# One boundary's work in another order on four engines, with re-shaped transfers, an earlier first slot and a moved loop turn, in a two-layer attention kernel

## The chip, the cores and the metric

The kernel runs on one core of a Trainium2 chip. The metric is the device time of one execution in microseconds (us), from loading the inputs to the last store of the output. Five engines run their own instruction streams in order: PE (matmuls), DVE and ACT (elementwise work and reductions), POOL (a slower elementwise engine) and SP, which here only issues DMAs. They are tied together by semaphores: an instruction increments one when it is done, another engine's stream waits until the count is reached. A stream never overtakes its own waiting instruction.

## What is computed

Eight images of 128 channels and 64 x 64 pixels pass through two layers.

```
# layer 0: wavelet split of x into four bands (32 x 32 each)
ll = (x1 + x2 + x3 + x4) / 2 ; lh, hl, hh = the three differences / 2
# low band: sparse attention, 8 heads of 16, N = 1024
q, k, v = qkv(ll);  q, k = q/|q|, k/|k|
attn = clip(q k^T * scale);  keep the 512 largest of each row, rest -1e9
ll_out = group_norm(proj(softmax(attn) v))
# three high bands: depthwise 3x3, group_norm, silu, 1x1 (384x384), group_norm
high = h + alpha * gn2(pw(silu(gn1(dw(h)))))
x_rec = inverse wavelet(ll + ll_out, high)
out = x + 0.1 * x_rec;  out = out + 0.1 * gn(w2 gelu(gn(w1 out)))
# layer 1: full attention over N = 4096 pixels with 16-wide q and k
q, k, v = Wq x + bq, Wk x + bk, Wv x + bv
x = gamma * (Wo (v softmax(q k^T / 4)^T) + bo) + x
```

## The kernel before, in words

The eight images form a pipeline of depth two. A stretch called `slots(b, l0, l1)` runs the eight heads of layer 0 of image b together with the eight chunks (512 queries each) of layer 1 of image b - 1. Between two such stretches stands `between(f, n, fin, opn)`: it finishes layer 0 of image f (`fin`: projection, group norms, ffn, and q, k, v of layer 1) and opens image n (`opn`: wavelet bands, q, k, v of layer 0, the convolutions of the high bands). There are nine such calls; the text calls them boundaries. The one that finishes image 0 is the first of eight that finish an image, and the fourth finishes image 3, at 2878 to 3050 us. The order of work on every engine is written out by hand, as a list of calls inside each engine's `between` and `slots`; every call contains its own waits. The same name on two engines (say `ffn1(3)`) is the two engines' share of one step.

**The turn of the loop.** Images 1 to 6 run in a hardware loop, `Fori(1, images - 1)`, whose body is `slots(b)` followed by `between(b, b + 1)`. The boundary after image 0 stands ahead of the loop and the last slots and boundary behind it. The loop turns back five times, from the end of a boundary to the start of the next slots.

**The end of the slots.** DVE masks the last exponentials of head 7 (line 1403), then copies the head's result out of PSUM (`head_out`, line 1456, tile OT; the rows 16, 48, 80 and 112 of OT hold the sums of the softmax). SP's `store_head` gathers those sums into OD (128 x 8, line 281) and stores the head to scrO (line 283); DVE's `sums` takes the reciprocal of OD (line 1462) and SP stores it to scrD (line 287). `load_done` reads all heads and reciprocals back as OC and OB, heads 0 to 6 first, head 7 at the boundary (lines 271, 276). Before `store_head` of head 7 SP issues that first `load_done` and, once head 7's masks are complete, the first half of the next image's x (`load_x`, line 243).

**The boundary.** `heads_out` (DVE, line 1632) multiplies OC by OB; `proj` (PE, line 647) projects; group norm 0 goes PE `group`, DVE `variance`, POOL `power`, PE `ungroup`, DVE `scales`; ACT `band0`, DVE `add0` give the new x (X1); `ffn1` (lines 682, 1029, 1691), group norm 3, `gelu` (line 1037), `ffn2` (lines 692, 1043, 1698), group norm 4, `norm2` and `add2` follow. Then `qk1`, `part1` (q and k of layer 1 split into three bf16 parts, PT1; the last is DVE line 1716, semaphore p12) and `values1`. Beside it, for the image that opens: POOL makes the bands out of x (`pairs`, `bands`, lines 1940 to 1968); `values0` (line 752), `qk0` (line 726) and `conv` (line 778) run on PE, the nine `taps` per band on DVE; `squares`, `clamp` and POOL's `norms` (a pow over 128 x 128, line 1975) and `repeat` (line 1981) give 1/|q| and 1/|k|; `spread` (PE, line 767) turns them and `normal` (DVE, line 1730) applies them; `part0` splits into bf16 parts; `silu` (line 1127), `points` (line 793) and `band` finish the high bands.

PE works in PSUM bank 4 for `qk0`, `values0`, `squares` and `spread`, one at a time.

**SP at the boundary.** `store_planes` writes the parts of layer 0 to scr0 (line 262, 12 DMAs of 256 KB), `load_head` reads the first three heads (line 255). Then X1 is stored to scrX (line 362, 2 MB), PT1 to scr1 (line 365, 3 x 256 KB, each row cut into its four places j), and q and k of layer 1 are read back as QP1 and KP1 (line 371, 7 DMAs, 1.5 MB); last the three high bands go to scrL (line 375).

**The first slot.** PE's `first` runs scores 2 to 7 of head 0 (line 428), then the 32 maxima products of chunk 0 (line 485), each in bank 4; DVE reduces each (line 1469) before the next one may start. The first of them waits for QP1 and KP1. ACT evicts the scores (line 905) and counts, for each of 1024 rows, the scores above a threshold (line 915); DVE's `update` (line 1272) moves the threshold after each round. In DVE's `first` the first four updates stand after maxima 5, 8, 13 and 17.

## Time and profile before

| | us |
|---|---|
| median of 3 runs | 6520.9 (6519.24 to 6528.7) |
| the profiled execution | 6521.32 |
| its span, first to last instruction | 6519.5 |
| PE busy | 4871.5 (75%) |
| DVE busy | 4702.5 (72%) |
| ACT busy | 4550.5 (70%) |
| POOL busy | 402.4 (6%) |
| mean granted clock of PE | 0.87 |

A profile is one execution on the chip. Times in it count from the span's start. Busy shares are averages over stretches with different limits. Idle time in brackets stands just before an instruction, with what ended it; it costs only where the engine is the one that everybody waits for. PEclk is PE's granted clock as a share of full speed. The DMA share is the mean busy share of the 16 DMA engines, so one engine at work all the time is 0.06.

### The profile page before, as it was taken

The numbers are of one execution on the slowest core, as the hardware profiler recorded it, in microseconds if no ns is written. First come the engines' busy times: TensorE is split into PE (matmuls) and PEld (weight loads), VectorE is DVE, ScalarE is ACT, GpSimd is POOL, SyncE is SP. The second block draws the span as 40 slices with busy tenths as digits, with TensorE's granted clock in tenths as the row PEclk, the third lists the DMA queues.
The fourth block names the chain that finished last, engine by engine and source line by source line (L and its number), as shares of the span: only waits on it lengthen the run. The fifth ranks groups of instructions, "written<-read, shape, count | busy, mean of one in ns | idle before, by whom it ended". The sixth has DMA issues, their size and how long they took to land.

```text
span 6519.5 us, 90843 instructions
## 1 busy us (share of the span) xinstructions
PE 4871.5 (75%) x30180; PEld 3041.3 (47%) x30180; DVE 4702.5 (72%) x8351; ACT 4550.5 (70%) x6907; POOL 402.4 (6%) x133
## 2 busy tenths in 40 slices
PE   4343688875888668875888758876788758884788
PEld 2000356542556335652556425553456425562566
DVE  3666588965998578975989659875898758983443
ACT  4884589945997469955999469964899459982223
POOL 3001100020000300011000200002000200000000
PEclk7555799986999879987999869997899869996899
DMA  1001100011001200011000110011000110001000
GB/s 59 6 9 44 64 13 14 13 49 66 13 18 40 74 12 16 15 51 64 13 16 35 41 50 18 16 52 64 9 18 13 48 64 15 18 33 36 9 7 12
DMA packets 97485, 199.95 MB, mean 31 GB/s; under 512 B 33960, under 2 KB 38952, under 8 KB 91336
## 3 DMA queue, kind: packets, MB, share of 16 engines
q1 hardware_dynamic: 96968, 193.57, 8.7%
q8 instruction: 261, 4.28, 0.3%
q14 instruction: 256, 2.10, 0.1%
HBM read 110.61 MB, written 82.05 MB: 30 GB/s over the span
## 4 chain that ended last, share of the span: by engine, by line
DVE 36%; issue 20%; PE 17%; ACT 11%; DMA 7%; POOL 5%; SPq 3%; DVEq 1%; ACTq 0%; POOLq 0%
DVE MX L1469 10%; ACT work L915 6%; PE PS L519 6%; DVE M L1325 6%; DVE arena L1403 6%; PE PS L485 4%; DVE work L1317 3%; DVE work L1285 3%; DVE work L1309 3%; DMA KP<-scr 3%; POOL RN L1975 3%; ACT work L933 2%; PE PS L457 2%; DMA scr<-arena 2%; SPq L262 1%
## 5 line engine op out<-in xcount | busy, mean ns | idle before, releaser
L915 ACT ACTIVATE work<-arena,T 128x1024 bf16<-128x1024 f32 x1792 | 2039.9, 1140 | 355.1 <-DVE T L1272 323.9
L519 PEld LDWEIGHTS PS<-V,work 128*128 128x128 f32 x16384 | 2017.7, 195 | 120.1 <-ACT work L940 29.2
L519 PE MATMUL PS<-V,work 128*128 128x129 f32 x16384 | 2045.8, 279 | 22.4 <-ACT work L940 22.4
L1469 DVE TENSOR_REDUCE MX<-PS 128x1 f32<-128x512 f32 x2048 | 1407.6, 687 | 743.3 <-PE PS L485 732.1
L485 PE MATMUL PS<-KP,QP 96*128 96x512 bf16 x2048 | 854.4, 417 | 646.3 <-DVE MX L1469 432.1
L940 ACT ACTIVATE work<-PS 128x1024 f32<-128x1024 f32 x1024 | 1039.7, 1015 | 406.4 <-PE PS L503 406.3
L485 PEld LDWEIGHTS PS<-KP,QP 96*128 96x128 bf16 x2048 | 200.9, 98 | 1215.5 <-DVE MX L1469 951.3
L1403 DVE SCALAR_TENSOR_TENSOR arena<-PS,work 128x1024 f32<-128x1024 f32 x512 | 624.6, 1220 | 194.1 <-ACT work L933 194.0
L503 PE MATMUL PS<-QP,KP 99*128 99x512 bf16 x2048 | 621.4, 385 | 60.1 <-ACT work L940 37.0
L905 ACT ACTIVATE arena<-PS 128x1024 f32<-128x1024 f32 x512 | 520.9, 1017 | 199.5 <-PE PS L428 198.4
L1325 DVE MAX8 M<-work 128x8 f32<-128x1024 f32 x512 | 625.5, 1222 | 3.0
L933 ACT ACTIVATE work<-PS 128x1024 f32<-128x1024 f32 x512 | 520.3, 1016 | 139.6 <-PE PS L457 136.3
L457 PE MATMUL PS<-work 99*128 99x512 bf16 x1024 | 336.9, 413 | 240.5 <-DVE arena L1403 185.4
L428 PE MATMUL PS<-work 96*128 96x512 bf16 x1024 | 362.5, 441 | 200.4 <-ACT arena L905 161.5
L1309 DVE TENSOR_SCALAR work<-arena,T 128x1024 f32<-128x1024 f32 x512 | 382.9, 748 | 23.7 <-DVE M L1325 5.7
L1317 DVE TENSOR_SCALAR work<-work,FL 128x1024 uint32<-128x1024 uint32 x512 | 376.4, 748 | 4.5
L915 ACT ACTIVATION_READ_ACCUMULATOR work<-arena,T 128x1 f32 x1792 | 343.4, 192 | 0.0
L1285 DVE TENSOR_SCALAR_CACHE_REDUCE work<-arena,T 128x1024 bf16<-128x1024 f32 x256 | 325.0, 1272 | 0.0
L503 PEld LDWEIGHTS PS<-QP,KP 99*128 99x128 bf16 x2048 | 182.3, 98 | 261.6 <-ACT work L940 89.5
L468 PE MATMUL PS<-arena,VT 128*17 128x256 f32 x4096 | 302.4, 408 | 0.0
L1940 POOL TENSOR_TENSOR work<-work 128x1024 f32<-128x1024 f32 x8 | 22.3, 2788 | 4383.2 <-DMA work<-in_x 4383.2
L457 PEld LDWEIGHTS PS<-work 99*128 99x128 bf16 x1024 | 66.0, 99 | 430.5 <-DVE arena L1403 355.0
(179 smaller groups left out, 3981.6 us busy)
## 6 DMA issues: line engine op xcount, KB each, us to landing
scr<-work SPq DMA_DIRECT2D x96, 256.0 KB
work<-scr SPq DMA_DIRECT2D x128, 192.0 KB, 2.7
work<-in_x SPq DMA_DIRECT2D x16, 1024.0 KB, 5.8
arena<-in_x SPq DMA_DIRECT2D x8, 2048.0 KB, 11.3
scrX<-arena SPq DMA_DIRECT2D x8, 2048.0 KB, 9.2
XR<-scrX SPq DMA_DIRECT2D x64, 256.0 KB, 2.7
out<-YO SPq DMA_DIRECT2D x64, 256.0 KB, 2.0
scrL<-work SPq DMA_DIRECT2D x24, 512.0 KB, 6.8
```

The costliest lines, as they stand in the source:

```text
L457: last = mm(PS[:, c, :], kp(h)[0:KA, 128 * mt:128 * mt + 128], qp(h)[0:KA, 512 * c:512 * c + 512], start=True, stop=True)
L485: mm(PS[:, 4, :], QP1[0:KS, c * 512 + 128 * i:c * 512 + 128 * i + 128], KP1[0:KS, 512 * w:512 * w + 512], start=True, stop=True).then_inc( ...
L503: last = mm(PS[:, 2 + t, :], KP1[0:KA, 128 * mt:128 * mt + 128], QP1[0:KA, j * 512:j * 512 + 512], start=True, stop=True)
L519: last = mm(PS[:, 5 + i // 2, 136 * (i % 2):136 * (i % 2) + 129], P1[:, (16 * j + k) % 3, t, 128 * i:128 * i + 128], V1[:, mt, :], start=( ...
L915: A(JKA[:, m % 2, :], scores(h, i), ACT.Sign, scale=-1.0, bias=T[:, h % 2, i:i + 1], accum_out=CA[:, h % 2, i:i + 1]).then_inc(s["ca"], 1)
L933: A(JA[:, mt % 2, :], bank2(0), ACT.Exp, scale=0.25).then_inc(s["e"], 1)
L940: A(P1[:, (16 * j + k) % 3, :, :].rearrange("p t n -> p (t n)"), PS[:, 2:4, :].rearrange("p a n -> p (a n)"), ACT.Exp, scale=0.25).then_in ...
L1309: cp.did(V.tensor_scalar(JD[:, c, :], scores(h, i), T[:, h % 2, i:i + 1], None, ALU.subtract))
L1317: cp.did(V.tensor_scalar(JDu[:, c, :], JDu[:, c, :], FL[:, h % 2, i:i + 1].bitcast(u32), None, ALU.bitwise_xor))
L1325: cp.did(V.max(M8[:, h % 2, i, :], JD[:, c, :]))
L1403: V.scalar_tensor_tensor(scores(h, mt), bank2(0), 0.0, JA[:, mt % 2, :], ALU.is_ge, ALU.mult)\
L1469: V.reduce_max(MX[:, c % 2, i, w:w + 1], PS[:, 4, :], AX.X).then_inc(s["mr"], 1)
```

## The change

Five things change.

1. Transfers. PT1 goes to scr1 row by row as it lies, and QP1 and KP1 are read with twelve DMAs of 16 rows (six pairs) in place of seven; scr1 becomes [3, 128, 1024]. The stores and loads now stand ahead of scrX's store. For heads 0 to 6 the gather of the sums is four DMAs, one per row of OT, in place of one. Head 7 has no gather: DVE takes the reciprocal of all of OT into a new tile OX, and SP stores its four rows.
2. SP issues the first `load_done` and the first half of the next x in head 7's slot right after the sums of head 6, ahead of the store of chunk 7.
3. The first slot. DVE's thresholds are updated between the first maxima (after 0, 3, 7, 11), and the four counts of round 2 and both their updates move from `search(0)` into `first`.
4. The loop's body is now the boundary `between(b - 1, b)` followed by `slots(b)`, so the loop turns back from the end of the slots to the start of a boundary; one boundary stands behind the loop.
5. The order of the calls in `between` on PE, ACT, DVE and POOL: the first value tile ahead of group norm 0, the second ahead of `ungroup(3)`, the spreads in one run ahead of the points, the first part of the second half's convolution ahead of ffn1; `repeat` ahead of `power(1)`.

The diff, cut to its core (the moved calls of `between` are shown for PE and, in part, for DVE, ACT and POOL):

```diff
@@ -103,7 +103,7 @@
-scr1 = nc.dram_tensor("scr1", [3, 32, N1], bf16, kind="Internal").ap()
+scr1 = nc.dram_tensor("scr1", [3, 128, N0], bf16, kind="Internal").ap()
...
@@ -263,10 +264,10 @@
...
     if first:
-        sp.wait_ge(s["od"], (b * NH + NH - 1) * 80)
+        sp.wait_ge(s["od"], b * OUTS + (NH - 1) * 128)
         rows, heads = slice(0, 112), slice(0, NH - 1)
     else:
-        sp.wait_ge(s["od"], (b + 1) * (NH * 80))
+        sp.wait_ge(s["od"], (b + 1) * OUTS)
         rows, heads = slice(112, 128), slice(NH - 1, NH)
...
@@ -278,13 +279,21 @@
...
     sp.wait_ge(s["o"], b * NH + h + 1)
-    sp.dma_start(OD[:, h % 2, :], OT[HD:128:32, h % 2, :].rearrange("q (j e) -> q j e", e=8)).then_inc(s["od"], 16)
+    if h < NH - 1:
+        for q in range(4):
+            sp.dma_start(OD[32 * q:32 * q + 32, h % 2, :],
+                         OT[32 * q + HD:32 * q + HD + 1, h % 2, :].rearrange("p (j e) -> p j e", e=8))\
+                .then_inc(s["od"], 16)
     for q in range(4):
-        sp.dma_start(scrO[h, :, 256 * q:256 * q + 256], OT[32 * q:32 * q + HD, h % 2, :]).then_inc(s["od"], 16)
+        sp.dma_start(scrO[h:h + 1, :, 256 * q:256 * q + 256].rearrange("h d n -> (h d) n"),
+                     OT[32 * q:32 * q + HD, h % 2, :]).then_inc(s["od"], 16)

...
     sp.wait_ge(s["rd"], b * NH + h + 1)
-    sp.dma_start(scrD[h:h + 1, :].rearrange("h (p e) -> (h p) e", e=8), ODR[:, h % 2, :]).then_inc(s["odr"], 16)
+    if h < NH - 1:
+        sp.dma_start(scrD[h:h + 1, :].rearrange("h (p e) -> (h p) e", e=8), ODR[:, h % 2, :]).then_inc(s["odr"], 16)
+    else:
+        sp.dma_start(scrD[h].rearrange("(q n) -> q n", q=4), OX[HD:128:32, :]).then_inc(s["odr"], 16)

...
@@ -317,12 +326,6 @@
...
             load_parts(b)
-        if l0 and h == NH:
-            load_done(b, True)
-            if more:
-                sp.wait_ge(s["p"], (b + 1) * (NH * NT))
-                sp.sem_inc(s["free"], 1)
-                load_x(b + 1, 0)
         if head(h):
...
@@ -341,6 +344,12 @@
...
             load_head(h + 3)
+        if l0 and h == NH - 1:
+            load_done(b, True)
+            if more:
+                sp.wait_ge(s["p"], (b + 1) * (NH * NT))
+                sp.sem_inc(s["free"], 1)
+                load_x(b + 1, 0)
         if chunk(h):
...
@@ -358,17 +367,16 @@
...
     if fin:
+        sp.wait_ge(s["p12"], f + 1)
+        for a in range(3):
+            sp.dma_start(scr1[a], PT1[:, a, :]).then_inc(s["scrw1"], 16)
+        sp.wait_ge(s["scrw1"], (f + 1) * 48)
+        for j, (tq, tk) in enumerate(TERMS):
+            for w, (t, dst) in enumerate(((tq, QP1), (tk, KP1))):
+                sp.dma_start(dst[16 * j:16 * j + 16].rearrange("p (j n) -> p j n", j=4),
+                             scr1[t].rearrange("(j s) n -> s j n", s=32)[16 * w:16 * w + 16]).then_inc(s["qp1"], 16)
         sp.wait_ge(s["x2"], (f + 1) * 4)
         sp.dma_start(scrX[bass.ds(f, 1)].rearrange("a c n -> c (a n)"), X1).then_inc(s["xs"], 16)
-        sp.wait_ge(s["p12"], f + 1)
-        for a in range(3):
-            sp.dma_start(scr1[a].rearrange("s (j n) -> j s n", j=4), PT1[:, a, :]).then_inc(s["scrw1"], 16)
-        sp.wait_ge(s["scrw1"], (f + 1) * 48)
-        q, k = scr1[:, 0:16, :], scr1[:, 16:32, :]
-        for dst, src in ((QP1[0:32], q[0].unsqueeze(0).to_broadcast([2, 16, N1])), (KP1[0:32], k[0:2]),
-                         (QP1[32:64], q[1].unsqueeze(0).to_broadcast([2, 16, N1])), (KP1[32:64], k[0:2]),
-                         (QP1[64:96], q[0:3:2]), (KP1[64:80], k[2]), (KP1[80:96], k[0])):
-            sp.dma_start(dst, src).then_inc(s["qp1"], 16)
     if opn:
...
@@ -381,10 +389,10 @@
...
 slots(0, True, False)
-between(0, 1, True, True)
 with sp.Fori(1, images - 1) as b:
+    between(b - 1, b, True, True)
     slots(b, True, True)
-    between(b, b + 1, True, True)
+between(images - 2, images - 1, True, True)
 slots(images - 1, True, True, False)
...
...
@@ -746,7 +754,7 @@
...
         else:
-            pe.wait_ge(s["qn"], n * 4 + 4)
+            pe.wait_ge(s["ssm"], n + 1)
         for m in range(4):
...
@@ -759,7 +767,7 @@
...
             pe.wait_ge(s["re"], n + 1)
-            pe.wait_ge(s["ssm"], n + 1)
+            pe.wait_ge(s["vt"], n * 2 + 2)
         else:
...
@@ -796,14 +804,15 @@
...
     proj(1)
+    values0(0)
     group(0)
-    values0(0)
+    qk0(0)
     ungroup(0)
     conv(0, 0, 0)
-    qk0(0)
     conv(0, 0, 1)
+    conv(0, 0, 2)
     qk0(1)
-    conv(0, 0, 2)
+    conv(0, 1, 0)
     qk0(2)
...
@@ -816,15 +825,15 @@
...
     ffn1(10)
+    qk0(3)
     ffn1(11)
     ffn1(12)
-    qk0(3)
     ffn1(13)
...
     group(3)
-    conv(0, 1, 0)
+    values0(1)
     ungroup(3)
...
@@ -834,23 +843,22 @@
...
     ffn2(5)
+    ffn2(6)
     group(1)
-    ffn2(6)
+    ffn2(7)
+    spread(0)
     ungroup(1)
-    spread(0)
     spread(1)
-    ffn2(7)
+    group(4)
     spread(2)
+    ungroup(4)
+    spread(3)
     points(0, 0)
-    spread(3)
     points(0, 1)
-    group(4)
-    values0(1)
     points(1, 0)
-    ungroup(4)
     points(1, 1)
+    values1(0)
     points(2, 0)
-    values1(0)
     points(2, 1)
...
...
@@ -1143,16 +1151,16 @@
...
     values0(0)
+    qk0(0)
     band0()
-    qk0(0)
     square(0)
...
     ffn1(2)
+    ffn1(3)
     qk0(2)
-    ffn1(3)
     ffn1(4)
...
@@ -1162,59 +1170,59 @@
...
     qk0(3)
+    square(3)
     ffn1(11)
     ffn1(12)
-    square(3)
     ffn1(13)
...
     ffn1(15)
+    values0(1)
     gelu(0)
...
     gelu(3)
+    conv(0, 0)
+    ffn2(0)
     gelu(4)
     gelu(5)
-    ffn2(0)
-    conv(0, 0)
+    ffn2(1)
     gelu(6)
     gelu(7)
-    ffn2(1)
     ffn2(2)
     ffn2(3)
-    conv(0, 1)
     ffn2(4)
     ffn2(5)
+    ffn2(6)
+    ffn2(7)
+    conv(0, 1)
     silu(0)
...
     part0(0, 0)
-    ffn2(6)
-    ffn2(7)
+    part0(0, 1)
+    norm2(0)
+    norm2(1)
+    points(0, 0)
     part0(1, 0)
-    part0(0, 1)
-    points(0, 0)
+    points(0, 1)
     part0(1, 1)
-    values0(1)
-    points(0, 1)
-    norm2(0)
+    norm2(2)
+    norm2(3)
     points(1, 0)
-    norm2(1)
-    norm2(2)
+    values1(0)
     points(1, 1)
-    norm2(3)
     points(2, 0)
-    values1(0)
+    points(2, 1)
     qk1()
...
     values1(1)
-    points(2, 1)
     values1(2)
     part1(1)
+    values1(3)
     band(0)
-    values1(3)
     values1(4)
+    values1(5)
     band(1)
-    values1(5)
     values1(6)
...
...
@@ -1452,13 +1460,18 @@
...
         if h >= 1:
-            dve.wait_ge(s["od"], (b * NH + h) * 80)
+            dve.wait_ge(s["od"], b * OUTS + h * 128)
         V.tensor_copy(OT[:, h % 2, :], PS[:, 7, 0:256]).then_inc(s["o"], 1)
+        if h == NH - 1:
+            dve.wait_ge(s["o"], (b + 1) * NH)
+            V.reciprocal(OX[:, :], OT[:, h % 2, :]).then_inc(s["rd"], 1)

...
             return
-        dve.wait_ge(s["od"], (b * NH + h + 1) * 80)
+        if h == NH - 1:
+            return
+        dve.wait_ge(s["od"], b * OUTS + h * 128 + 128)
         V.reciprocal(ODR[:, h % 2, :], OD[:, h % 2, :]).then_inc(s["rd"], 1)
...
...
@@ -1504,30 +1517,54 @@
...
         centre(0, 1)
-        for k in range(24):
+        update(0, 0, 0)
+        for k in range(3):
             maxima(0, k)
-            if k in (5, 8, 13, 17):
-                g = (5, 8, 13, 17).index(k)
-                update(0, g // 2, g % 2)
+        update(0, 0, 1)
+        for k in range(3, 7):
+            maxima(0, k)
+        update(0, 1, 0)
+        for k in range(7, 11):
+            maxima(0, k)
+        update(0, 1, 1)
+        for i in range(4):
+            count(0, 2, 4 + i)
+            maxima(0, 11 + i)
+        update(0, 2, 0)
+        update(0, 2, 1)
+        for k in range(15, 30):
+            maxima(0, k)

     def search(h):
-        count(h, 2, 4)
-        maxima(h, 24)
+        if h >= 1:
+            count(h, 2, 4)
+        if h >= 1:
+            maxima(h, 24)
         mask(h - 1, 3)
-        count(h, 2, 5)
-        maxima(h, 25)
-        count(h, 2, 6)
-        maxima(h, 26)
...
@@ -1790,81 +1827,81 @@
...
     add0(2)
+    taps(1, 0)
     add0(3)
-    taps(2, 0)
-    taps(1, 0)
-    taps(2, 1)
+    taps(1, 1)
+    conv(0, 0)
     ffn1(0)
+    taps(1, 2)
     ffn1(1)
     ffn1(2)
-    taps(1, 1)
-    conv(0, 0)
     ffn1(3)
-    taps(1, 2)
+    taps(2, 0)
     ffn1(4)
+    taps(2, 1)
     ffn1(5)
...
     ffn1(8)
-    taps(1, 3)
     ffn1(9)
+    taps(2, 2)
     ffn1(10)
-    taps(1, 4)
+    taps(2, 3)
     ffn1(11)
...
     moments(3)
+    taps(2, 4)
     clamp()
     variance(3)
+    taps(2, 5)
+    taps(1, 3)
+    scales(3)
+    taps(1, 4)
     taps(1, 5)
-    taps(2, 2)
-    scales(3)
-    taps(2, 3)
-    taps(2, 4)
     taps(1, 6)
-    taps(2, 5)
     taps(1, 7)
+    taps(2, 6)
     taps(1, 8)
-    taps(2, 6)
+    conv(0, 1)
     taps(2, 7)
-    conv(0, 1)
-    taps(2, 8)
+    ffn2(0)
     conv(1, 0)
     conv(1, 1)
+    taps(2, 8)
+    ffn2(1)
     conv(2, 0)
+    ffn2(2)
     conv(2, 1)
+    ffn2(3)
     moments(1)
+    ffn2(4)
     variance(1)
-    ffn2(0)
+    ffn2(5)
+    ffn2(6)
+    ffn2(7)
+    normal(0)
+    moments(4)
     scales(1)
-    ffn2(1)
-    normal(0)
-    ffn2(2)
-    ffn2(3)
-    ffn2(4)
     normal(1)
-    ffn2(5)
+    variance(4)
+    normal(2)
+    normal(3)
+    scales(4)
+    points(0, 0)
+    add2(0)
     part0(1, 0)
-    normal(2)
-    ffn2(6)
+    points(0, 1)
+    part0(1, 1)
     part0(2, 0)
-    ffn2(7)
-    points(0, 0)
-    normal(3)
-    moments(4)
-    part0(1, 1)
-    points(0, 1)
     part0(2, 1)
-    variance(4)
-    scales(4)
     points(1, 0)
+    add2(1)
     points(1, 1)
-    add2(0)
-    add2(1)
+    add2(2)
     points(2, 0)
-    add2(2)
     add2(3)
...
...
@@ -2000,8 +2037,8 @@
...
     norms()
+    repeat()
     power(f, n, fin, opn, 1)
-    repeat()
     power(f, n, fin, opn, 4)
...
@@ -2012,13 +2049,14 @@
...
 between(0, 0, False, True)
-between(0, 1, True, True)
 with pool.Fori(1, images - 1) as b:
-    between(b, b + 1, True, True)
+    between(b - 1, b, True, True)
+between(images - 2, images - 1, True, True)
 between(images - 1, images, True, False)
...
 DSET = 15
+OUTS = (NH - 1) * 128 + 64

...
```

## Rows read from the trace of the kernel before

**Rows 1.** Waits, all engines: waiter <- releaser: us in total, times, longest us.
```profile
PE PS L485 <- DMA KP<-scr: 172.5, 7, 38.6
...
PE PS L428 <- issue: 32.0, 5, 6.5
```

**Rows 2.** Chain of work, 2870 to 3060 us: start, us, what.
```profile
2880.08 9.39 DMA work<-in_x
...
3024.09 25.56 DMA KP<-scr
```

**Rows 3.** SP timeline, DMA issues of a slot and the fourth boundary.
```profile
2785.81 1.86 SPq L283 DMA_DIRECT2D scrO<-OT  x4
...
2793.89 0.34 SPq L287 DMA_DIRECT2D scrD<-ODR  x1
...
2881.14 2.35 SPq L283 DMA_DIRECT2D scrO<-OT  x4
2890.66 0.34 SPq L287 DMA_DIRECT2D scrD<-ODR  x1
...
2892.08 0.58 SPq L276 DMA_DIRECT2D work<-scrD  x1
2978.90 13.97 SPq L262 DMA_DIRECT2D scr<-work  x12
...
3002.96 5.67 SPq L365 DMA_DIRECT2D scr<-arena  x3
3020.25 0.69 SPq L371 DMA_DIRECT2D QP<-scr  x1
```

**Rows 4.** Windows: busy PE, PEld, DVE, ACT, POOL; PEclk, DMA share, GB/s.
```profile
3004.00:3006.00 2.00, 0.51 (x5) 0.32 (x3) 0.00 (x0) 1.55 (x2) 0.00 (x0) 1.00 1.06 424
...
3014.00:3016.00 2.00, 0.79 (x3) 0.13 (x2) 0.00 (x0) 1.11 (x2) 0.00 (x0) 0.50 0.26 100
...
3038.00:3040.00 2.00, 0.00 (x0) 0.00 (x0) 0.00 (x0) 0.00 (x0) 0.00 (x0) 0.50 0.14 57
```

**Rows 5.** PE timeline, fourth boundary: start, us, engine, line, what [idle <-releaser].
```profile
2896.34 3.71 PE L647 MATMUL PS<-work,w_proj 128*128 128x512 f32 x4 [18.14 <-DVE work L1632]
...
2904.36 2.08 PE L752 MATMUL PS<-w_qkv,work 128*128 128x128 f32 x8 [1.87 <-POOL work L1958]
...
2921.10 11.32 PE L682 MATMUL PS<-arena,w 128*128 128x512 f32 x26
...
3011.00 1.03 PE L428 MATMUL PS<-work 96*128 96x512 bf16 x2 [6.49 <-issue]
...
3049.70 0.61 PE L485 MATMUL PS<-KP,QP 96*128 96x512 bf16 x1 [21.75 <-DMA KP<-scr]
```

**Rows 6.** DVE timeline, fourth boundary; last row: the last boundary's first maxima.
```profile
2878.27 0.42 DVE L1456 COPY OT<-PS 128x256 f32<-128x256 f32 x1 [0.27 <-PE PS L468]
...
2894.51 1.77 DVE L1632 TENSOR_TENSOR work<-work 128x1024 f32<-128x1024 f32 x1 [3.88 <-DMA work<-scrD]
...
2999.55 1.23 DVE L1716 TENSOR_TENSOR arena<-arena 128x1024 bf16<-128x1024 f32 x1 [0.72 <-ACT arena L1066]
...
6018.67 0.69 DVE L1469 TENSOR_REDUCE MX<-PS 128x1 f32<-128x512 f32 x1 [41.63 <-PE PS L485]
```

**Rows 7.** POOL timeline: first boundary's start, fourth boundary's pow.
```profile
627.75 2.79 POOL L1940 TENSOR_TENSOR work<-work 128x1024 f32<-128x1024 f32 x1 [517.62 <-DMA work<-in_x]
...
2942.16 21.66 POOL L1975 TENSOR_TENSOR RN<-SSM,mhalf 128x128 f32<-128x128 f32 x1
```

**Rows 8.** ACT timeline, fourth boundary: the silus, the last count.
```profile
2966.23 3.50 ACT L1127 ACTIVATE work<-work,SHH,SCH 128x1024 f32<-128x1024 f32 x3 [3.79 <-DVE SHH L1676]
...
3032.83 1.13 ACT L915 ACTIVATE work<-arena,T 128x1024 bf16<-128x1024 f32 x1
```

**Rows 9.** The page, part 6, x loads: count, KB each, median us to landing.
```profile
work<-in_x SPq DMA_DIRECT2D x16, 1024.0 KB, 5.8
```

**Rows 10.** PE timeline, first boundary: its first maxima matmul.
```profile
786.26 0.61 PE L485 MATMUL PS<-KP,QP 96*128 96x512 bf16 x1 [27.07 <-DMA KP<-scr]
```

41 lines of the change are left out of this document (28 added, 13 removed).

## The prediction, written before the change was run

> **What bounds the kernel now.** I read the list of waits first, then the chain of work around one boundary between images (2870 to 3060 us, the fourth of eight), then the timelines of SP, PE, DVE, ACT and POOL there, and last the windows for what the DMA engines did. The waits name two PE stalls that happen only at boundaries: the first maxima matmul (line 485) waits 172.5 us in seven boundaries for the KP1/QP1 loads, and the first score matmul (line 428) sits 6.5 us five times with nothing to wait for, once per turn of the loop [rows 1]. The chain shows how much of a boundary is transfer: 9.39 us for the next image's x and 25.56 us for the KP1 loads [rows 2]; the scr1 stores, issued from 3002.96, hold the loads back until 3020.25 [rows 3]. The windows explain both. While SBUF row tiles move whole (3004 to 3006), the share of the 16 DMA engines is 1.06 at 424 GB/s; while the scr1 stores drain (3014 to 3016) it is 0.26, four engines' worth; during the KP1/QP1 loads (3038 to 3040) it is 0.14 at 57 GB/s, about two engines' worth [rows 4]. The stored pattern leads with 4 (j), most of the loads lead with 2. So width follows the leading dimension, and PE idles 21.75 us behind two engines [rows 5].
>
> **Where one loop boundary spends its time.** In us of the fourth boundary: head 7 copied out at 2878.69, heads_out starts 2894.51 [rows 6], x has landed at 2889.47 [rows 2], the low band is ready about 2904.3, ffn1 starts 2921.10 [rows 5], the pow of the norms runs 2942.16 to 2963.82 [rows 7], silu starts 2966.23 [rows 8], the layer-1 parts (p12) are complete at 3000.78 [rows 6], the first maxima matmul runs at 3049.70 [rows 5]. From there 32 maxima ping-pong between PE and DVE, and nothing overtakes them. The first maxima is therefore the milestone; its gain is the image's gain.
>
> **Part 1, transfers of the head output and of x.** Before, the x half (1 MB) is issued at 2880.08, just ahead of head 7's stores, and these (issued by 2883.49) let the reciprocal and its store go only at 2890.66 [rows 2, 3]. After, the x half is issued as soon as the last mask is done, some 2873.1: it lands 5.8 us (the page's median, [rows 9]) later or somewhat sooner, at 2878 to 2879. x is 10.5 to 11 us earlier, so the low band is ready near 2893.2 instead of 2904.3. Head 7's four stores go out at about 2878.8 onto quiet queues; SP is done with them by 2880.7 and they land by 2882.2 (1.5 us later, an estimate from the small gaps on quiet queues). The gather OD and the small reciprocal are gone; one reciprocal of 128x256 on DVE replaces them (0.42 us if it runs like the copy of that size in [rows 6], 1.4 us if its cost per element is larger; both are over before SP has issued the four stores). The two loads then follow, and as before heads_out starts 1.85 us after the last one is issued [rows 3, 6]. That gives heads_out at about 2885.2, 9.3 us earlier.
>
> **Part 2, the order of the boundary**, walked with the durations of the same trace. PE does proj (3.7 us from 2896.34, [rows 5]), then the value tile first: it waits for the low band until 2893.2, 2.1 us [rows 5], and the group matmul behind it starts at 2895.2, behind its own turn by some 2 us. DVE's variance then follows without POOL beside it, and ungroup ends near 2898.4, 9.6 us earlier. The convolution of the second half now stands ahead of ffn1 (2.74 us more, 1 us of qk less): ffn1 starts about 2914.2, 6.9 us earlier. ffn1 is paced by DVE: 16 statistics of 0.6 us and 5 taps of 1.2 us, 15.5 us in all; before, it was one tap less and one statistic more, much the same. taps(2,4) ahead of clamp costs 1.2 us, the second value tile takes the place of 4.5 us of convolution before ungroup: gelu starts 7.5 us earlier and the pow at 2936.5, 5.7 us earlier. The pow is unchanged at 21.66 us [rows 7]. Repeat (1.88 us) now runs ahead of the band norm's power, and normal(0) and moments(4) stand before scales(1) on DVE: silu starts at about 2963.6, only 2.6 us earlier. Behind it the order pays. All four spreads and the value tile are done while ACT runs silu (3.50 us, [rows 8]), and the six pointwise products run back to back (6 x 2.7 us, one value tile between); before, three spreads, a value tile and ffn2 stood between them. p12 comes at 2991.8, 9.0 us earlier. PE ends the values about 2995 and ACT about 2996.5. The six head loads are no limit: twelve plane stores take 13.97 us of SP [rows 3], now from 2969.2, and land about 2988.2.
>
> **Part 3, the loop turn.** It moves from before the scores to before heads_out, where PE waits anyway. The 6.49 us [rows 5] go from PE's path. SP now turns between the store of the sums and the loads. No row shows SP's turn; its bounds are 0 and PE's 6.5. A late heads_out is half hidden by the 2 us wait for the low band, so at most 3.2 us a boundary are lost; I take half, 1.6, in five boundaries: 8 us.
>
> **Part 4, scr1.** SP is free at p12 and nothing of scrX is in front. Three stores at 1.16 us each (13.97 / 12, [rows 3]) and about 2.5 us to land: 2997.8. Twelve loads at 0.62 us each (the first took 0.69, [rows 3]) are issued by 3005.2 and land 1.85 us later, about 3007 (9.3 us after the first issue). The other bound is the rate of the four-engine rows: 1.5 MB at 100 GB/s, 15 to 16 us, about 3014 [rows 4]. I take the first, since both sides of each load now lead with 16. PE meanwhile runs the eight scores: they start at ACT's pace near 2996.5 and end at 3011.5. So PE, no longer the load, is late, and the first maxima matmul goes at 3011.5: 38.2 us earlier. The scrX store moves behind the loads; its readers are the XR loads and the eviction of head 1, some 70 us later, which hide it.
>
> **Part 5, first slot.** The thresholds no longer wait for maxima, so ACT idles less. But ACT was ahead anyway; the ping-pong sets the end, and the four DVE counts only change place. A small cost appears: update(0,0,1) stands after three maxima (4.2 us), and ACT's eighth count ends 6.1 us after the last score (before: 3033.96 [rows 8] against 3027.95, where PE's 21.75 us of idling begin [rows 5]). DVE waits 1.8 us, with PE's next maxima behind it. Net per loop boundary: 38.2 - 1.8 = 36.4 us. The others differ by fractions from the fourth; I use 36.1.
>
> **The other boundaries.** In the first one x was early already (POOL starts at 627.75, 3.8 us after the head copy [rows 7]), so value tile and convolution ahead of their old places cost: p12 2.3 us later. Its first maxima goes from 786.26 after 27.07 us of idling [rows 10] to about 761.6: 24.7 less 1.8, 22.9 us. In the last, without a next image, heads_out comes 6.5 us earlier (896 KB no longer ahead of the stores), and p12 to first maxima shrinks from 41.0 us (DVE idled 41.63, [rows 6]) to 14.0 us: 33.5 us together. In the slots SP issues three more gathers per head (1.9 us); the sums wait until 2793.89, 6.2 us after the last store of 2785.81 was issued [rows 3], which hides it at no cost; without that cover it costs DVE up to 1.9 us a head.
>
> **Sum:** 22.9 + 6 x 36.1 + 33.5 - 8 = 265 us. The profiled execution took 6521.3 us (span 6519.5); the median of 6520.9 stands 0.4 below. 6521 - 265 = 6256 us.
>
> What a page says of the width: the Trainium skill, DMA: Bandwidth & Descriptors, section "Why a DMA increments its semaphore by 16 and not by 1", lets a transfer run on the largest number of engines up to 16 that divides the leading sizes of both sides. By that rule it is 4 and 2 engines before, and the trace agrees (0.26, 0.14 [rows 4]). By the same rule it is 16 for the new stores and loads, which no row shows, and the sum would be the one above; with rival B it would be wrong.
>
> **Rivals.**
> A, the loads are wide but slow, at 100 GB/s for 16 target partitions (the four-engine rate, [rows 4]). The loads then land 3014 to 3016.5 and eat the 1.8 us too: about 1.5 us in each of six boundaries, 2 in the first, 7 in the last: 18 us, 6274 us. For it: no row here fills 16 partitions with much data. Against: that rate came with four engines. A page speaks for it: SBUF — State Buffer, section "Door 1: The DMA port swizzle" of the Trainium skill, says that bandwidth goes by the SBUF ports that the partitions reach, 27.2 GB/s each; by that page 16 partitions reach 4, an estimate of 109 GB/s and 14 us for 1.5 MB. No run so far shows it.
> B, the transfers don't get wider, so the change doesn't do what it says. 3 stores and loads then take about 35 us from p12: maxima near 3027, 22.7 us gained in six boundaries, 9 in the first, 13 in the last: 158 us, 6363 us. Against: head loads and x with 96 and 128 leading rows do fill the engines.
> C, the order gives nothing: the wait for the low band ahead of group and the pow ahead of spreads and silu eat what x and heads_out give, p12 stays put. 9 us in six boundaries: 54 us less, 6310 us. For it: silu gains only 2.6 us in my walk.
> D, slower than before: the gathers of heads 0 to 6, now four transfers each out of one partition, land late and DVE waits in sums, with masks and maxima behind it. Price: the 56 heads would have to lose 265 / 56 = 4.7 us each, so gathers would have to land 4.7 + 4.3 = 9 us after the last store instead of within 6.2. Beyond 9 us the kernel is slower; at 10 it takes 6575 us. Against: 128 pieces of 32 bytes per head, as before.
>
> **How the numbers follow.** Forecast 0.55, A 0.25 (6274), C 0.10 (6310), B 0.07 (6363), D 0.03. The forecast's own range is 6228 (no SP turn, each boundary 3 us better) to 6280. The range 6228 to 6315 takes in A and C. Faster by over 0.2% (13 us, about what a measurement of this kernel can tell from no change): all but D and a sliver, 0.96; same 0.01; slower 0.03.
>
> **What would show it.** After: no wait of line 485 on KP loads over 3 us except in the last boundary; a DMA share well above 0.14 right after p12; 8 to 10 us from head copy to heads_out; the wait before line 428 without its 6.5 us; silu start to p12 28 us instead of 34.5; pow unchanged at 21.66 and starting about 58 us after the head copy instead of 63.5; DVE's sums without a wait in heads 0 to 6. A first maxima that still waits 5 to 10 us on loads says A, 15 or more B; p12 more than 112 us after heads_out says C (I expect 106.6; before, 106.3). What would make it wrong: a wait in the new order that my walk of four queues missed, multiplied by six.

## The result, and the profile after

The changed kernel takes 6239.9 us (median of 4 runs, 6235.4 to 6247.7) against 6520.8 us: ratio 0.9568, 95% interval 0.9552 to 0.9585, 281 us less. The forecast was 6256 (range 6228 to 6315). The profiled execution took 6235.5 us (span 6233.7), so between the two profiled executions lie 285.8 us. Medians here are of fast runs: one of the four runs of the kernel with the scr1 transfers alone took 6938.4 us at a granted clock of 0.69 and isn't counted.

Page of the changed kernel, busy times and the chain by engine:

```profile
PE 4879.6 (78%) x30180; PEld 3049.5 (49%) x30180; DVE 4693.0 (75%) x8351; ACT 4554.4 (73%) x6907; POOL 401.2 (6%) x133
...
DVE 32%; PE 21%; issue 19%; ACT 18%; POOL 4%; DMA 3%; SPq 2%; DVEq 0%; ACTq 0%; POOLq 0%
```

In its list of waits (total, times, longest) the KP loads are down from 172.5 us to 16.9, of which 15.4 stand in the last boundary, and no row is left for the turn of the loop at the first score [rows 1]:

```profile
DVE MX L1482 <- PE PS L493: 537.8, 699, 18.4
...
PE PS L655 <- DVE work L1669: 80.3, 8, 12.4
...
PE PS L493 <- DMA KP<-scr: 16.9, 2, 15.4
```

SP at the fourth boundary (start, duration, what was issued). The x half goes out 5 us ahead of the head copy (which ends at 2777.83), then come the head's stores and the sums; the loads for heads_out are issued at 2782.97 and 2783.42. 2.2 us lie between the two pairs, the wait for the stores and SP's loop turn:

```profile
2772.32 0.35 SPq L244 DMA_DIRECT2D work<-in_x  x1
...
2777.86 2.27 SPq L288 DMA_DIRECT2D scrO<-OT  x4
2780.17 0.58 SPq L296 DMA_DIRECT2D scrD<-OX  x1
2782.97 0.32 SPq L272 DMA_DIRECT2D work<-scrO  x1
2783.42 0.54 SPq L277 DMA_DIRECT2D work<-scrD  x1
```

SP at the end of the same boundary, where p12 is complete at 2891.51: three stores, 4.5 us, and twelve loads at 0.47 us from start to start.

```profile
2891.54 1.32 SPq L372 DMA_DIRECT2D scr<-arena  x3
2896.04 0.33 SPq L376 DMA_DIRECT2D QP<-scr  x1
...
2901.09 0.43 SPq L376 DMA_DIRECT2D KP<-scr  x1
2901.81 0.37 SPq L379 DMA_DIRECT2D scrX<-arena  x1
```

PE there. Scores run from 2894.43, the last at 2910.51, and the first maxima matmul follows with no wait. In the row of before it waited 21.75 us [rows 5]:

```profile
2894.43 0.60 PE L436 MATMUL PS<-work 96*128 96x512 bf16 x2
...
2910.51 1.03 PE L436 MATMUL PS<-work 96*128 96x512 bf16 x2 [1.21 <-ACT arena L913]
2911.34 0.63 PE L493 MATMUL PS<-KP,QP 96*128 96x512 bf16 x1
```

Windows of the same stretch (last two columns: share of the 16 DMA engines and GB/s; the one before is PE's granted clock). The loads have all engines busy, but move only 115 GB/s, where [rows 4] had 424 with the same share:

```profile
2892.00:2894.00 2.00, 1.61 (x15) 1.46 (x14) 0.00 (x0) 2.00 (x5) 0.00 (x0) 1.00 1.03 354
...
2902.00:2904.00 2.00, 0.79 (x3) 0.13 (x2) 0.17 (x1) 1.38 (x3) 0.00 (x0) 0.50 1.05 115
2904.00:2906.00 2.00, 0.58 (x2) 0.00 (x0) 0.00 (x0) 2.00 (x5) 0.00 (x0) 0.50 1.07 115
```

Only the last boundary, where no scores stand in front, still shows how long the loads take: first issue at 5720.25, first maxima at 5734.57, 14.3 us.

```profile
5720.25 0.33 SPq L376 DMA_DIRECT2D QP<-scr  x1
```
```profile
5734.57 0.59 PE L493 MATMUL PS<-KP,QP 96*128 96x512 bf16 x1 [15.36 <-DMA KP<-scr]
```

Times of the milestones behind the end of the last head copy (us), worked out from the timelines (heads_out and silu: their start; p12: the end of the last part; first maxima: the start of the matmul); "fourth" is the boundary of the working:

| | heads_out | silu | p12 | first maxima |
|---|---|---|---|---|
| first, before / after | 8.3 / 7.2 | 79.4 / 85.3 | 115.3 / 113.5 | 161.9 / 133.3 |
| fourth, before / after | 15.8 / 8.0 | 87.5 / 81.6 | 122.1 / 113.7 | 171.0 / 133.5 |
| last, before / after | 12.5 / 5.9 | none | 89.4 / 81.4 | 130.4 / 99.2 |

The first maxima gains 28.6 us in the first boundary, 36.4, 38.1, 37.5, 37.7, 39.4 and 38.0 in the next six and 31.2 in the last: 286.9. Before the first boundary 3.0 us are lost, the slots lose 0.5 and the end gains 2.3: 285.7 of the 285.8. The gain is all at the boundaries.

### The profile page after: what moved, and what is told of

Same layout as the page of the kernel before. It is cut to its first block, busy times and chain, and to the rows that moved or that the text cites. A ratio compares the mean times of both kernels' runs of the same rounds, so it can differ in the third digit from the quotient of the medians.

```text
span 6233.7 us, 91139 instructions
## 1 busy us (share of the span) xinstructions
PE 4879.6 (78%) x30180; PEld 3049.5 (49%) x30180; DVE 4693.0 (75%) x8351; ACT 4554.4 (73%) x6907; POOL 401.2 (6%) x133
## 4 chain that ended last, share of the span: by engine, by line
DVE 32%; PE 21%; issue 19%; ACT 18%; POOL 4%; DMA 3%; SPq 2%; DVEq 0%; ACTq 0%; POOLq 0%
ACT work L923 10%; DVE MX L1482 9%; PE PS L527 6%; DVE M L1333 5%; DVE arena L1411 5%; PE PS L493 4%; ACT work L941 3%; DVE work L1325 3%; POOL RN L2012 3%; DVE work L1293 3%; DVE work L1317 2%; ACT work L948 2%; PE PS L465 2%; PE PS L801 2%; PE PS L786 1%
## 5 line engine op out<-in xcount | busy, mean ns | idle before, releaser
L1317 DVE TENSOR_SCALAR work<-arena,T 128x1024 f32<-128x1024 f32 x512 | 383.1, 748 | 19.7 <-DVE M L1333 0.5
## 6 DMA issues: line engine op xcount, KB each, us to landing
scrX<-arena SPq DMA_DIRECT2D x8, 2048.0 KB, 14.5
```

## The experiments

Kernels are told by what they change against the changed kernel, unless the text says otherwise. One warning on size: the four runs of the changed kernel spread over 12 us, those of one experiment (two queues) over 30. The experiments ran on four chips, each beside the kernel before (6522.7 to 6524.8 us there) but not beside the changed kernel. A difference under some 10 us between two medians is not explained here unless a row of the trace carries it.

**The scr1 transfers alone**, put into the kernel before:

```diff
-scr1[a].rearrange("s (j n) -> j s n", j=4) <- PT1[:, a, :]      # leads with 4
+scr1[a] <- PT1[:, a, :]                                         # leads with 128
-QP1[0:32], KP1[0:32], ... <- scr1 (leads 2)                     # 7 loads
+for j: QP1[16j:16j+16], KP1[16j:16j+16] <- scr1 (leads 16)      # 12 loads, scrX behind them
```

> The kernel before with the scr1 transfers of the change alone (row-shaped stores, twelve loads of 16 rows, the scrX store behind them); order, loop turn, x and first slot as before. My theory (the wide transfers are hidden behind the scores, and the stall of the first maxima was theirs alone): in each boundary the wait of the first maxima on the KP1 loads goes, 27.1 us in the first, 20 to 22.5 in the next six, 23 in the last (p12 to first maxima 41.0 to 17.7 us), together some 180 us, 6341 us; p12 stays about 122 us behind the head copy. Rival (the 37.5 us of a loop boundary are mainly the order and the loop turn): gain below 100 us, over 6420 us, with a wait of 10 us or more left before the first maxima. In neither the loads' rate rises: about 115 GB/s with all 16 engines busy, not 424.

Measured 6331.2 us (ratio 0.9706, interval 0.9687 to 0.9726), 191.5 less than the kernel before on the same chip. No wait on the loads is left but the last boundary's 15.95 us, and p12 stays where it was or comes up to 2 us later (122.2 to 124.2 us behind the copy in the loop, 122.0 to 122.7 before). In the five boundaries with a turn of the loop, p12 to first maxima is 23.4 to 25.2 us: the turn of the loop still stands there, and scores, not loads, are last. Two thirds of the whole gain are this one edit.

**The next image's x and the load of seven heads back at their old place:**

> The changed kernel with the next image's first x half and the load of seven finished heads at their old place (ahead of the last head's stores instead of a head earlier). Theory: x lands 10.5 us later, heads_out some 4 us later (the half moves in front of the head's stores), p12 6 to 7 us later in six boundaries and 3 in the last: 6275 to 6285 us. Rival (x is not on the path with the new order): heads_out decides alone, p12 4 us later or less, under 6262 us.

Measured 6323.2 us (ratio 0.9695, interval 0.9679 to 0.9711): 83 us are lost, twice the expectation. DVE and PE of its fourth boundary (head copy ended 2802.76):

```profile
2818.35 3.23 DVE L1669 TENSOR_TENSOR work<-work 128x1024 f32<-128x1024 f32 x1 [13.80 <-DMA work<-scrD]
```
```profile
2821.63 3.78 PE L655 MATMUL PS<-work,w_proj 128*128 128x512 f32 x4 [19.36 <-DVE work L1669]
2829.76 2.07 PE L760 MATMUL PS<-w_qkv,work 128*128 128x128 f32 x8 [4.35 <-POOL work L1995]
```

heads_out is 7.6 us later (15.6 against 8.0) and takes 3.23 us. In the changed kernel it took 1.23 there, but 1.2 to 3.3 over the eight boundaries, with GpSimd's passes beside it in both kernels; what makes the difference is open. The value tile, which stands first in the new order, waits 4.35 us for the late low band (1.48 in the changed kernel) with the group matmul behind it. ffn1 starts 46.4 behind the copy instead of 33.1, and p12 comes 8 to 17 us later in the six boundaries between the first and the last, as much as heads_out (7.6 to 9.3) or more. So the 7.8 us by which heads_out came earlier are the place of x and of the seven heads' load, not the head's own transfers. The two were moved together. In the last boundary there is no next x, and there the load's place alone makes 5.1 us (heads_out at 11.0 instead of 5.9).

**The old transfers of a head's sums:**

```diff
-for q in range(4): OD[32q:32q+32, ...] <- OT[32q+HD:32q+HD+1, ...]    # heads 0 to 6
+OD[:, ...] <- OT[HD:128:32, ...]                                       # one gather, all 8 heads
-V.reciprocal(OX, OT[:, h % 2, :]); scrD[h] <- OX[HD:128:32, :]         # last head
```

> The changed kernel with the old transfers of a head's sums (one gather of three-partition pieces, small reciprocal, one row store, also for the last head). Theory: in the slots the one gather costs or saves nothing; at the boundary the last head's sums go out a landing and a small reciprocal later, heads_out 2 to 3 us later than 8.0 behind the head copy, of which half is hidden by the wait for the low band: 6248 to 6262 us. Rival (the 7.8 us by which heads_out came earlier are this edit's own): heads_out at 14 us or more, 6285 us or more.

6235.1 us (ratio 0.9557, interval 0.9542 to 0.9571), no loss at all. heads_out is 2 to 3 us later as expected (9.9 to 10.8), yet in the fourth boundary ffn1 starts earlier (31.4 for 33.1) and p12 is at 110.6 for 113.7. In the last boundary the changed kernel's form is worth 3.6 us at p12 (81.4 for 85.1). The slots take the same 583.0 us, so the gathers of heads 0 to 6 cost nothing. Its PE at the fourth boundary, and the changed kernel's:

```profile
2788.66 3.72 PE L646 MATMUL PS<-work,w_proj 128*128 128x512 f32 x4 [12.55 <-DVE work L1655]
2792.22 1.05 PE L751 MATMUL PS<-w_qkv,work 128*128 128x128 f32 x8
...
2795.92 7.99 PE L777 MATMUL PS<-PAD,diag 128*128 128x512 f32 x18
```
```profile
2787.10 3.78 PE L655 MATMUL PS<-work,w_proj 128*128 128x512 f32 x4 [9.76 <-DVE work L1669]
2792.36 2.07 PE L760 MATMUL PS<-w_qkv,work 128*128 128x128 f32 x8 [1.48 <-POOL work L1995]
...
2797.63 9.15 PE L786 MATMUL PS<-PAD,diag 128*128 128x512 f32 x18
```

With heads_out later the value tile has nothing to wait for and runs in 1.05 us instead of 2.07, the convolutions in 7.99 instead of 9.15: PE's granted clock is back at 1.00 from 15.6 us behind the copy, in the changed kernel from 22.2. The earlier heads_out of the changed kernel was paid back by a wait and a half clock.

**The old order of the boundary's work** on all four engines:

> The changed kernel with the old order of the boundary's work on PE, ACT, DVE and POOL, everything else of the change kept. Theory (the order is worth what stands between heads_out and p12, 106.3 before and 105.7 after): 0.6 us a boundary at p12 and 0.6 more up to the end of the scores, 6244 us at most; heads_out 8.0 us behind the head copy, p12 within 115. Rival (the order carries the 8.4 us by which p12 comes earlier, since only it uses the early x): p12 at 120 to 122 us behind the copy, 6285 to 6295 us.

6230.6 us (ratio 0.9553, interval 0.9537 to 0.9569; 6227.3 to 6231.5, below every run of the changed kernel). So the order of the change gains nothing. Whether it costs something isn't shown: the medians are 9 us apart, but the first maxima of the two profiled executions differ by 2.6 us over all eight boundaries. Silu starts at 76.3 to 78.0 (80.1 to 81.8 in the changed kernel), 2.4 us behind the end of the pow instead of 5.3, and p12 is at 110.1 to 114.0 although it has the old 34 to 36 us from silu to p12.

**Silu's scales ahead of repeat and the first spread again**, then also **one pointwise product between the spreads**:

```diff
 norms(); -repeat(); power(1); +repeat()                       # GpSimd
 -normal(0); -moments(4); scales(1); +normal(0); +moments(4)   # DVE
 ffn2(7); +ungroup(1); spread(0); -ungroup(1); ...             # PE
 spread(2); +points(0, 0); ungroup(4); spread(3); -points(0, 0)   # second kernel only
```

> The changed kernel with the scales of the band norm ahead of repeat, of the first spread and of normal(0) on GpSimd, PE and DVE, as before the change; the spreads still in one run behind it. Theory: silu starts 2.4 us behind the end of the pow, as before (78.8 instead of 81.7 us behind the head copy), but the four spreads in one run still end after it and at half clock: points start no earlier than about 87, p12 at most 1 us earlier, 6231 to 6240 us. Rival (silu alone holds up the points): points and p12 3 us earlier, 6215 to 6222 us.

> As the one before it, and the first pointwise product stands between the third and the fourth spread on PE. Theory (the run of small matmuls, 128 columns each, is what the half clock of 10 us comes from and goes with): points start at 83 to 84 instead of 87.9, the granted clock is back at 1.0 some 5 us earlier, p12 at 109 to 110.5 instead of 113.7, 6205 to 6220 us. Rival (the clock falls all the same, the stall is DVE's between the spreads): p12 113 or later, within 5 us of the one before it.

6243.5 us (0.9554 to 0.9584) and 6256.4 us (0.9573 to 0.9602). The first did in the boundaries what its theory said, though its time is 3.5 us above the range: silu at 79 to 81, points no earlier (86.4 to 89.2, 85.4 to 88.0 in the changed kernel), p12 no earlier (112.4 to 115.2, against 110.0 to 113.9). The second missed: points do start at 83.5 to 86.7, but p12 stays at 113.2 to 115.9. The granted clock still falls at about 80 us behind the copy in five of the six boundaries, and is back at 87 to 89 instead of 89 to 91. Only in the fourth does PE keep it through the spreads. There the third product waits 2.03 us for ACT, whose eviction of the first stands behind the normalised last tile and two norm2, and the clock falls there instead (granted clock is the third number from the end):

```profile
2884.26 7.11 PE L801 MATMUL PS<-work,w_pw 128*128 128x512 f32 x12 [2.03 <-ACT work L1144]
```
```profile
2882.00:2884.00 2.00, 0.23 (x1) 0.00 (x0) 1.37 (x2) 2.00 (x3) 0.00 (x0) 1.00 0.29 36
2886.00:2888.00 2.00, 2.00 (x4) 0.85 (x3) 2.00 (x3) 1.81 (x4) 0.00 (x0) 0.50 0.53 187
```

So its theory isn't borne out: the clock falls in five boundaries with the product between the spreads, and in two of the changed kernel's it stays up without it. Some 6 us of its loss stand before the first head copy, in the first image, and aren't explained.

**The old loop turn:**

> The changed kernel with the loop turn where it was (ahead of the scores). Theory: PE's 6.5 us come back before the first score in five boundaries, heads_out comes 1.5 us earlier (SP does not turn between the sums' store and the loads) and p12 with it at most as much: 5 x 5.0 to 6.5 us, 6261 to 6268 us. Rival (the KP1 loads are so close behind the scores that they were the end, and the turn is hidden by them): less than 2 us a boundary, under 6246 us.

6253.8 us (ratio 0.9584, interval 0.9568 to 0.9600), 14 us lost, between the two expectations. SP's turn is 2.1 us: heads_out comes at 5.9 instead of 8.0. PE's turn is back, but as an idle time of 3.35 us in the fourth boundary (3.1 to 3.7 in the loop; 3.4 to 4.7 in the kernel with the scr1 transfers alone, 6.3 to 6.5 before, in the fourth 6.49 [rows 5]); what makes it shorter isn't shown:

```profile
2904.88 0.60 PE L436 MATMUL PS<-work 96*128 96x512 bf16 x2 [3.35 <-issue]
```

p12 to first maxima is 22.5 to 23.0 us in the loop's boundaries instead of 19.8. But with heads_out 2.1 us earlier, and the clock at 1.00 through the spreads in four of these five boundaries (in one of the changed kernel's), the first maxima come only 1 us later in the five together. The loss is in the slots (first maxima to the next last head copy), which take 585.0 to 585.9 us instead of 583.2. Of this, 0.8 to 2.4 us a slot lie between the second and the third head copy: 67.6 to 69.3 us, against 66.8 in the changed kernel. The kernel before and the one with the scr1 transfers alone have the longer time too, also in the slots ahead of which nothing has turned yet. Why is open.

**The old first slot** (DVE's thresholds behind six, nine, fourteen and eighteen maxima):

> The changed kernel with the old order of DVE's thresholds and maxima in the first slot. Theory (the ping-pong of 32 maxima sets the slot's end; first maxima to the next image's last head copy took 583.5 us before and after): 6230 to 6243 us, at best 1.2 to 1.8 us a slot gained because the second threshold does not wait for ACT's counts. Rival (ACT idles for thresholds and the rest of the slot follows it): 3 us or more a slot, over 6260 us.

6222.6 us (ratio 0.9542, interval 0.9529 to 0.9555), 17 us faster than the changed kernel, more than expected. Rows of DVE, changed kernel and this one:

```profile
2915.75 0.69 DVE L1482 TENSOR_REDUCE MX<-PS 128x1 f32<-128x512 f32 x1 [0.70 <-PE PS L493]
2917.68 0.16 DVE L1280 SCALAR_TENSOR_TENSOR T<-CA,T 128x4 f32<-128x4 f32 x1 [1.24 <-ACT work L923]
```
```profile
2913.85 0.69 DVE L1482 TENSOR_REDUCE MX<-PS 128x1 f32<-128x512 f32 x1 [0.70 <-PE PS L493]
2914.46 0.15 DVE L1280 SCALAR_TENSOR_TENSOR T<-CA,T 128x4 f32<-128x4 f32 x1
```

The threshold waits for ACT in the first and not in the second. This wait is not all: at the thirty-second maxima the changed kernel is 1.0 us behind (46.6 against 45.7 us after the first), at the next head copy 2.2. The counts of round 2 were moved back by the same edit, so the rest is not put down to one of the two. First maxima to the next last head copy is 580.7 to 581.0 us in five images of the loop, where the changed kernel has 583.2 or 583.3 in four and 580.2 in one: 2.3 us in four images, some 9 us. Another 3 lie in the first maxima of the boundaries, which no edit of this kernel explains. Together that is the 13 us between the two profiled executions; the medians' 17 hold 4 more that no trace shows. Both were tried together as well (old order and old first slot):

> The changed kernel with both the old order of the boundary's work and the old first slot: only transfers, the place of x and the loop turn are of the change. Theory (the two are independent: 9.3 us and 17.3 us too much in the changed kernel): 6213 us, 6206 to 6220. Rival (both only shift the clock's falls, and the sum does not hold): 6222 us or more.

6227.8 us (0.9535 to 0.9561): the sum doesn't hold. The slots keep their 2.3 us, but in four boundaries the first maxima waits 0.8 to 2.3 us for the loads: in this order they, not the scores, are last. The scores end about where they did, 19.7 to 20.6 us behind p12 (19.7 to 20.0 in the changed kernel). The loads are later, because the first goes out 5.5 to 7.2 us behind p12 in all boundaries but the last (3.4 to 4.8 in the changed kernel, but for one boundary). SP's rows of its fourth boundary show why (p12 is complete at 2884.33): six head loads are issued until 2885.17, and the scr1 stores land behind them:

```profile
2882.50 2.67 SPq L256 DMA_DIRECT2D work<-scr  x6
2885.21 1.43 SPq L372 DMA_DIRECT2D scr<-arena  x3
2890.82 0.33 SPq L376 DMA_DIRECT2D QP<-scr  x1
```

With the old first slot the old order is 5 us slower (6227.8 for 6222.6), with the new one 9 us faster. Within the spread of these runs the order is worth nothing either way.

**Two queues for the loads**, KP1 issued by GpSimd:

> The changed kernel with the six KP1 loads issued by GpSimd on its own queue, from the last 16 partitions down, beside the six QP1 loads on SyncE's, from the first 16 up. Theory (115 GB/s is what a transfer into 16 partitions gets at a time, the engines only wait for it; two transfers into different partitions at once get twice that): in the last boundary, where nothing hides the loads, first issue to first maxima falls from 14.3 us to 8 to 10, the wait of the first maxima from 15.4 to 9 to 11; the other boundaries stay as they are, 6230 to 6238 us. Rival (the 16 DMA engines themselves are full, their share is 1.07): 14 us as before, whatever the queues.

6236.3 us (0.9548 to 0.9577). The last boundary waits 15.50 us (15.36 before), first issue (5699.26) to first maxima is 14.5 us. Issuing is over in 3.6 us instead of 5.5, and the engines are full again:

```profile
5704.00:5706.00 2.00, 0.00 (x0) 0.00 (x0) 0.00 (x0) 0.00 (x0) 0.00 (x0) 0.50 1.12 140
5708.00:5710.00 2.00, 0.00 (x0) 0.00 (x0) 0.00 (x0) 0.00 (x0) 0.00 (x0) 0.50 1.10 278
```

Not a clean test: the 2 MB scrX store was issued at 5701.97, 2.7 us behind the first load instead of 5.5, and from another queue than KP1's, so it shares the engines with them. In this test the loads land no sooner; whether two transfers into different partitions could, is open.

**Maxima between the scores.** On old order and old first slot: the loads split so that what the first maxima need lands first, and three maxima stand between scores 4 to 7.

```diff
-for k in range(32): maxima(0, k)                     # behind scores 2 to 7
+for i in range(5, 8): maxima(0, i - 5); score(0, i)
+for k in range(3, 32): maxima(0, k)
 # loads: KP1, quarter of QP1 | rest of QP1, waited for by the third chunk
```

> As the one before, and the loads split so that KP1 and the first quarter of QP1 land first (the other three quarters behind, waited for by the third chunk), with the first three maxima woven between the last scores. Theory (12 of the loads' 18 parts, 0.96 of 1.5 MB, stand before the first maxima, and the scores are ACT's pace with PE and DVE half idle): first maxima 5 us earlier against the last head copy, the thirty-second 4.2 us earlier in seven boundaries, 5 us in the last: 6213 less 34, some 6180 us. Rival (the thresholds and counts behind the eighth score bound the slot, or the maxima hold the scores back): under 10 us gained on the kernel before it.

6205.6 us (0.9496 to 0.9522), 22 us less than the kernel it builds on: two thirds of the expectation. The first maxima comes earlier, but still waits 2.5 to 5.1 us (11.1 in the last boundary), and three scores now stand behind it:

```profile
2894.38 0.61 PE L496 MATMUL PS<-KP,QP 96*128 96x512 bf16 x1 [5.07 <-DMA QP<-scr]
```

**A quarter of both first:**

> As the one before (maxima woven between the last scores), and KP1 split too: the first quarter of QP1 and of KP1 (0.4 MB) land first and free the first two maxima, the other three quarters of KP1 free the third, those of QP1 the third chunk. Theory (at 115 to 125 GB/s the first twelve transfers land some 8 us behind their first issue instead of 10.5, and score 5 no longer stands behind a wait of 2.5 to 5 us): the wait before the first maxima under 1 us in seven boundaries, first maxima some 3 us earlier, 6205 less 7 x 3 and 4 in the last, 6180 us. Rival (transfers of 32 KB cost an engine as much as those of 128 KB, or the third maxima now waits what the first did): under 8 us gained, over 6197 us.

6190.5 us (ratio 0.9489, interval 0.9476 to 0.9502; 6186.2 to 6193.4): another 15 us, of 25 expected. The wait is 0 to 1.8 us in seven boundaries and 7.88 in the last, and a small one now stands before the third maxima:

```profile
2883.20 0.61 PE L499 MATMUL PS<-KP,QP 96*128 96x512 bf16 x1 [1.81 <-DMA KP<-scr]
...
2887.81 0.61 PE L499 MATMUL PS<-KP,QP 96*128 96x512 bf16 x1 [0.90 <-DMA KP<-scr]
```

This version is 49 us faster than the changed kernel and 334 us faster than the one before it on the same chip (6190.5 against 6524.8).

## Why the prediction held, point by point

**Bound and milestone: right.** The sum went by the first maxima of each boundary; 286.9 us are there, against 285.8 in all. The total was 20.8 us short, and this is where. The six boundaries between the first and the last were forecast at 208.6 us together (6 x 36.1, less 8) and gave 227.2, 36.4 to 39.4 each. Of this, 7.8 us are at the first maxima, where the forecast had 219.4 (6 x 37.9, less 8); the rest is the 1.8 us a slot that it took off again and that the slots didn't show. The first boundary was forecast at 22.9 and gave 28.6, less 3.0 lost ahead of it, which no step had. The last boundary's 33.5 came out as 33.5 by luck: 8.0 us up to p12 instead of 6.5, 23.2 from p12 to the first maxima instead of 27.0, and 2.3 behind it, which no step had.

**Part 4: result right, one term wrong by a half.** The width was read rightly: share 1.05 to 1.10 of 16 engines instead of 0.14. By the rule of the Trainium skill (DMA: Bandwidth & Descriptors, "Why a DMA increments its semaphore by 16 and not by 1") 16 engines were to be expected; the trace agrees. The step that failed is "land 1.85 us later, about 3007 (9.3 us after the first issue)": it took 14.3 us. That is close to the other bound (15 to 16 us) and to rival A's 100 GB/s; the windows have 115 to 127. The Trainium skill's SBUF — State Buffer, "Door 1: The DMA port swizzle", puts 16 partitions at about 109 GB/s, an estimate of 14 us for the 1.5 MB; the time agrees, and the 115 to 127 GB/s of the windows lie somewhat above that rate. It cost next to nothing, because stores and latency took 4.5 us instead of 6.0 and the scores ended 19.8 us behind p12 (forecast 19.7): the last load lands 18.1 to 19.5 us behind p12 by the trace's semaphore events, 0.3 to 1.8 us ahead of the first maxima, and in the fourth boundary 0.3. One boundary, the fifth, shows the edge, a wait of 1.56 us. There "the six head loads are no limit" failed: p12 is early (110.0), SP issues head loads until 0.9 us behind it, and the first QP1 load goes out 6.8 us behind it. So A's mechanism was real and its price of 18 us wrong, as it let the loads land 22 to 25 us behind p12.

**Part 1: right in size, and the size is what was issued earlier.** heads_out came 7.8 us earlier, and 9.8 with the loop turn moved back (forecast 9.3; SP's turn was in Part 3). The old-x kernel gives the whole of the 7.8 to the place of x and of the seven heads' load, and shows that this place matters more than my walk allowed: 83 us. The reciprocal of 128x256 took 1.75 us, above my upper bound of 1.4, hidden behind the stores all the same. The heads' own transfers turned out worth 3.6 us in the last boundary and nothing in the whole.

**Part 2: p12 right (8.4 us against 9.0), the reason wrong.** "Behind it the order pays" is the step that failed. The walk had silu gain 2.6 us and silu to p12 shrink from 34.5 to 28.2. Measured are 6.0 and 32.1: one error of 3.4 us and one of 3.9 that cancel, which is luck. The first is in front of the pow, which started 54.6 us behind the copy, not 58. With the old order silu is 10 us earlier than before, 4 to 5 earlier than in the changed kernel, and p12 is no later. The early p12 is that of the transfers and of their place; the new order gives back at silu (behind repeat, the first spread and normal(0)) and ahead of ffn1 what it wins behind silu. The working had "all four spreads and the value tile are done while ACT runs silu". They were not: silu ended at 2862.9, the last spread at 2865.9. Behind the first, each spread took 2.08 us instead of 1.16, at a granted clock of 0.50, which the working did not allow for. In the first and the fifth boundary the clock stayed at 1.00, and there silu to p12 is 28.2 us, just what the walk had. So the term that failed behind silu is the clock, not the count of work. The second spread in the fourth and in the fifth boundary, and the fourth boundary's windows:

```profile
2858.09 2.08 PE L775 MATMUL PS<-cons,work 128*128 128x128 f32 x8
```
```profile
3575.01 1.16 PE L775 MATMUL PS<-cons,work 128*128 128x128 f32 x8
```
```profile
2856.00:2858.00 2.00, 1.85 (x14) 1.71 (x14) 1.10 (x3) 1.49 (x2) 0.52 (x2) 1.00 0.00 0
2858.00:2860.00 2.00, 1.98 (x9) 1.78 (x8) 1.18 (x8) 0.62 (x1) 0.00 (x0) 0.50 0.00 0
...
2866.00:2868.00 2.00, 2.00 (x3) 0.68 (x3) 0.98 (x4) 1.37 (x2) 0.00 (x0) 0.50 0.00 0
```

Rival C ("the order gives nothing") was right in what it says of the order, and wrong in its price, because it let the order eat the gain of x and heads_out too. The sign named for it, p12 more than 112 us behind heads_out, couldn't tell: in the fourth boundary it is 105.7 with the new order and 104.1 with the old.

**Part 3: small as forecast.** SP's turn is 2.1 us, 1.6 were taken. But that 6.49 us a boundary go from PE's path overrates it: once the transfers are changed, PE's turn is an idle time of 3.1 to 4.7 us. With the old loop p12 to first maxima is 3.1 us longer and heads_out 2.1 earlier, so in the five boundaries little is left of either. The 14 us that the old loop costs are for the most part the unexplained 2 us a slot, which no step had.

**Part 5: right in size.** Forecast a wait of 1.8 us a slot; the old first slot is 2.3 us a slot better, of which 1.0 is there when the maxima end. Against the kernel before, the thirty-second maxima is 1.8 us later behind the first (46.6 for 44.8). The slots as a whole didn't get longer (583.2 before and after); the 2 us that the loop turn's new place is worth there would just cover it, which is an argument from two experiments and not a measurement.

**D and B** didn't come: the reciprocal of the sums shows no wait on a DMA in heads 0 to 6, and the share is 1.07.

## What to carry to other kernels

Find the work that stands last at a stage's end and ask what it will be once the first wait is gone: here the loads took half as long again as forecast (14.3 us for 9.3). Where scores stand in front it didn't matter as long as the loads went out up to 4.8 us behind p12; where they went out 5.5 us or more behind it, the first maxima waited up to 2.3 us. An order by hand is worth testing apart from the transfers it came with: here it is most of the diff and gains nothing, and the new first slot, which costs 2.3 us a slot, was hidden in the same change. The next gain lay in letting a chain (maxima) start inside the work that covers its data, with the data split by who needs it first.
